# Self-attention of a transformer block: four first-pass banks, and row sums inverted in a layout over all partitions

## What is computed

```python
xn = layer_norm(x, ln0_w, ln0_b)
q, k, v = split(xn @ qkv_w.T)              # each as 16 heads x 32
attn = einsum('bhnd,bhmd->bhnm', q, k) * 32 ** -0.5
attn = softmax(attn)                       # 2048 keys a row
sa = merge(einsum('bhnm,bhmd->bhnd', attn, v)) @ sa_proj_w.T
x = x + sa
```

## Time and profile before

| | |
|---|---|
| median of 3 runs | 3681.93 us (3677.66 to 3685.92) |
| the profiled execution | 3683.99 us, its span 3682.2 us |
| TensorE (PE) busy | 3365.0 us, 91% of the span |
| VectorE (DVE) busy | 2215.5 us, 60% |
| GpSimd (POOL) busy | 1701.3 us, 46% |
| ScalarE (ACT) busy | 1545.2 us, 42% |
| maxima, L1591 | 2048 of 676 ns, 1277.9 us |
| exponentials, L1549 | 2048 of 603 ns, 1068.0 us |
| pair sums, L1397 | 192 of 4598 ns and 64 of 4579 ns |
| accumulating DMAs, L1402 | 128 of 1024 KB, 7.2 us to landing |

### The profile page before, as it was taken

One profiled execution on the slowest core, in us unless ns is written; L12 is line 12 of the kernel. 1 busy time (PEld: TensorE's weight loads), 2 busy tenths in 40 slices (PEclk: granted clock), 3 DMA queues, 4 the chain that ended last, 5 costly groups with the idle time before them and its releaser, 6 DMA issues. The chain is left out here.

```text
span 3682.2 us, 52183 instructions
## 1 busy us (share of the span) xinstructions
PE 3365.0 (91%) x16432; PEld 2104.9 (57%) x16432; DVE 2215.5 (60%) x3731; ACT 1545.2 (42%) x2794; POOL 1701.3 (46%) x507
## 2 busy tenths in 40 slices
PE   7998999999999999999999668898876689999999
PEld 6885544444444444444444156556535568888887
DVE  4445878887888888888888125666644632222222
ACT  3230666666666666666666512442422321111111
POOL 0001788888888888888878622342322200000000
PEclk9997999999999999999999887898957889999999
DMA  4547347465465746546553453333315741111110
GB/s 171 180 163 183 71 100 161 87 133 116 96 131 107 155 86 140 115 97 131 107 118 74 106 146 95 116 112 108 90 53 206 263 163 46 46 46 46 46 46 23
DMA packets 178499, 412.01 MB, mean 112 GB/s; under 512 B 20289, under 2 KB 43399, under 8 KB 158831
## 3 DMA queue, kind: packets, MB, share of 16 engines
q1 hardware_dynamic: 156271, 273.87, 24.4%
q0 software_dynamic: 18432, 134.23, 18.2%
q10 hardware_dynamic: 3584, 1.05, 0.1%
HBM read 146.08 MB, written 102.56 MB: 68 GB/s over the span
## 5 line engine op out<-in xcount | busy, mean ns | idle before, releaser
L1591 DVE TENSOR_REDUCE self_part_max<-self_first 128x1 f32<-128x512 f32 x2048 | 1277.9, 676 | 299.9 <-PE self_first L1448 296.6
L1549 ACT ACTIVATE self_expo<-self_second 128x512 f32<-128x512 f32 x2048 | 1068.0, 603 | 690.0 <-PE self_second L1464 656.4
L1397 POOL TENSOR_TENSOR self_pair_sum<-self_expo 128x2048 f32<-128x2048 f32 x192 | 882.8, 4598 | 117.4 <-ACT self_expo L1549 93.9
L1448 PE MATMUL self_first<-self_k,self_q 96*128 96x512 f32 x2048 | 884.6, 439 | 40.9 <-DVE self_part_max L1591 24.2
L1464 PE MATMUL self_second<-self_q,self_k 98*128 98x512 f32 x2048 | 813.4, 400 | 13.5 <-ACT self_expo L1549 13.4
L1448 PEld LDWEIGHTS self_first<-self_k,self_q 96*128 96x128 f32 x2048 | 394.6, 193 | 559.1 <-DVE self_part_max L1591 445.2
L1477 PE MATMUL self_weighted<-self_expo,self_v_sb 128*32 128x512 f32 x4096 | 546.3, 605 | 9.1 <-ACT self_unscaled L1561 6.9
L1464 PEld LDWEIGHTS self_second<-self_q,self_k 98*128 98x128 f32 x2048 | 388.5, 190 | 109.6 <-ACT self_expo L1549 47.7
L1943 DVE CAST mlp_h_high<-mlp_h 128x512 fp32r<-128x512 f32 x128 | 54.7, 427 | 505.6 <-PE mlp_out_sum L61 504.6
L1918 ACT ACTIVATE mlp_h<-mlp_hidden_sum,mlp_b_col 128x512 f32<-128x512 f32 x128 | 88.0, 688 | 601.1 <-PE mlp_hidden_sum L61 601.1
L1397 POOL TENSOR_TENSOR self_half_sum<-self_expo 128x2048 f32<-128x2048 f32 x64 | 292.7, 4579 | 82.9 <-ACT self_expo L1549 82.9
(11 more groups left out here) (165 smaller groups left out, 4130.7 us busy)
## 6 DMA issues: line engine op xcount, KB each, us to landing
self_half_sum<-self_pair_sum POOLq DMA_DIRECT2D x128, 1024.0 KB, 7.2
self_k<-k_t SPq DMA_DIRECT2D x96, 256.0 KB, 9.7
self_q<-q_t SPq DMA_DIRECT2D x93, 256.0 KB, 4.5
cross_q<-cross_r_high SPq DMA_DIRECT2D x256, 64.0 KB, 2.0
qkv_x<-in_x SPq DMA_DIRECT2D x8, 1024.0 KB, 5.4
v<-qkv_v_sb SPq DMA_DIRECT2D x32, 256.0 KB, 2.0
q_t<-qkv_r_high SPq DMA_DIRECT2D x32, 256.0 KB, 2.0
q_t<-qkv_r_low SPq DMA_DIRECT2D x32, 256.0 KB, 2.3
```

The source lines that it names most:

```text
L1397: nc.gpsimd.tensor_tensor(to, expo[:, t % p_slots], expo[:, (t + 1) % p_slots], ALU.add).then_inc(pair_done, 1)
L1448: nc.tensor.matmul(first[:, in_ring[n]], q[0:base, c % q_slots, a, s * P:(s + 1) * P], k[0:base, c // stages_per_group % 2, a, k0:k0 + TOK ...
L1549: nc.scalar.activation(expo[:, t % p_slots, a], second[:, n % ring], ACT.Exp, scale=scale).then_inc(exp_done, 1)
L1591: nc.vector.tensor_reduce(part_max[:, a * SUB + s, k:k + 1], first[:, in_ring[n]], AX_X, ALU.max).then_inc(first_read, 1)
```

## The change

It has three parts.

1. **Banks.** The first pass gets four banks (`f_ring`), the second keeps three (`s_ring`), `weighted` keeps one, and `total` has none of its own. The transposed maximum and `total` now take slots of the second pass's ring (`s_uses` lists the ring's uses in order; `second_free` waits for the use three places back). The transpose stands between first-pass items 0 and 1 (`turn_after = 1`).
2. **Sums.** The three sums stand in a row behind block 3. ScalarE copies `weighted` straight into `mean` (block 1, once the last `mean` is stored) and `total` into `inverse` in SBUF (`take_total`, behind exponential 15). Since sums and overwritten buffers have moved, GpSimd's `part_sum` has four parts whose roles alternate by stage.
3. **Inversion.** One row of each head is sent by four small DMAs from `inverse` into `sums`, a tensor of 128 partitions x 16 columns (`send_sums`). VectorE inverts that in one instruction in block 7. SyncE stores it to DRAM (`spread_inverse`), waits for this, and loads each head's 512 values into 32 partitions of `inverse` by a broadcast DMA, four in all. VectorE divides in block 11: `inverse` times `mean`, both in SBUF. SyncE then stores `mean`.

The maxima's two DMAs stay behind block 13 (`max_sent_after = 55`).

```diff
-    turn_after = 2
-    ring = 3
+    turn_after = 1
+    f_ring = 4
+    s_ring = 3
...
-    sums_at = {15: [(0, 0)], 2: [(-1, 1)], 3: [(-1, 2)]}
-    last_sum, invert_from, max_sent = 3, 5, 13
+    sum_block, take_sum_after = 3, 4 * per_block - 1
+    invert_at, divide_at, max_sent_after = (7, 1), (11, 1), 55
...
+    s_uses = []
+    for j in range(blocks):
+        for at in range(per_block):
+            if first_of[j][at] == (2, turn_after - 1):
+                s_uses.append("turn")
+            s_uses.append(j * per_block + at)
+        if j == sum_block:
+            s_uses.append("total")
+    s_slot = {use: p % s_ring for p, use in enumerate(s_uses)}
...
-        first = m.psum("first", [P, ring, TOK])
-        second = m.psum("second", [P, ring, TOK])
+        first = m.psum("first", [P, f_ring, TOK])
+        second = m.psum("second", [P, s_ring, TOK])
         weighted = m.psum("weighted", [P, TOK])
-        total = m.psum("total", [P, TOK])
+        total = second[:, s_slot["total"]]
+        turned_max = second[0:n_max, s_slot["turn"], 0:P]
...
+                def send_sums(i):
+                    ge(sp, total_read, i + 1, alone=True)
+                    for a in range(heads):
+                        rows = slice(a * HEAD_DIM, (a + 1) * HEAD_DIM)
+                        sp.dma_start(sums[rows], inverse[a * HEAD_DIM:a * HEAD_DIM + 1].rearrange("o (j k) -> o j k", k=share)
+                                     ).then_inc(sums_loaded, 16)
+
+                def spread_inverse(i):
+                    ge(sp, inverse_done, i + 1, alone=True)
+                    sp.dma_start(inverse_rows.rearrange("a (j k) -> (a j) k", k=share), sums[:]).then_inc(inverse_stored, 16)
+                    ge(sp, inverse_stored, 16 * (i + 1), alone=True)
+                    for a in range(heads):
+                        sp.dma_start(inverse[a * HEAD_DIM:(a + 1) * HEAD_DIM],
+                                     inverse_rows[a].unsqueeze(0).to_broadcast([HEAD_DIM, TOK])).then_inc(inverse_loaded, 16)
...
+                    if number != 0:
+                        send_sums(i - 1)
                     v_free(0)
                     if number != 0:
+                        spread_inverse(i - 1)
+                    v_free(1)
+                    if number != 0:
                         store_out(r, c - 1)
-                    v_free(1)
                     v_free(2)
...
+                def take_total(i):
+                    ge(act, total_done, n_sums * (i + 1))
                     ge(act, mean_done, i)
-                    nc.scalar.activation(unscaled[:], weighted[:], ACT.Copy).then_inc(weighted_read, 1)
+                    nc.scalar.activation(inverse[:], total, ACT.Copy).then_inc(total_read, 1)
...
+                def invert(i):
+                    ge(dve, sums_loaded, 16 * heads * (i + 1))
+                    nc.vector.reciprocal(sums[:], sums[:]).then_inc(inverse_done, 1)
 
                 def divide(i):
-                    ge(dve, inverse_done, pieces * (i + 1))
+                    ge(dve, inverse_loaded, 16 * heads * (i + 1))
                     ge(dve, weighted_read, i + 1)
-                    ge(dve, out_stored, 16 * i)
-                    nc.vector.tensor_tensor(mean[:], total[:], unscaled[:], ALU.mult).then_inc(mean_done, 1)
+                    nc.vector.tensor_tensor(mean[:], inverse[:], mean[:], ALU.mult).then_inc(mean_done, 1)
```

More of the change, by code:

```diff
@@ L1197, in self_phase @@
     n_seconds = heads * n_k
-    blocks = n_k
-    per_block = heads
+    blocks = 16
+    per_block = n_seconds // blocks
     firsts_per_block = n_items // blocks
     ahead = per_head
-    turn_after = 2
-    ring = 3
+    turn_after = 1
+    f_ring = 4
+    s_ring = 3
     p_slots = 8
-    pieces = 8
+    share = heads * TOK // P
     k_set = n_k // 4
@@ L1213, in self_phase, with sum_parts @@
     n_adds = n_pairs + 1
[L1214 to L1215 removed]
+    sum_block, take_sum_after = 3, 4 * per_block - 1
+    invert_at, divide_at, max_sent_after = (7, 1), (11, 1), 55
     items = [(a, s, k0) for a in range(heads) for s in range(SUB) for k0 in range(0, keys, TOK)]
[L1218 to L1240 removed]
+    def sum_parts(c):
+        return (0, 1, 2, 3) if c % 2 == 0 else (2, 1, 0, 3)
     first_of = [[] for _ in range(blocks)]
@@ L1381, in _ @@
                     period(rounds - 1, c)
+                send_sums(stages - 1)
+                spread_inverse(stages - 1)
                 store_out(rounds - 1, round_stages - 1)
@@ L1461, in second_pass @@
                         ge(pe, max_loaded, 32 * (i + 1))
-                    held = n - ring if n >= ring else (n_seconds - 1 - n) // ring * ring + n - n_seconds
-                    ge(pe, exp_done, n_seconds * i + held + 1)
-                    nc.tensor.matmul(second[:, n % ring],
+                    second_free(i, n)
+                    nc.tensor.matmul(second[:, s_slot[n]],
                                      k[0:exp_rows, c // stages_per_group % 2, a, t * P:(t + 1) * P],
@@ L1503, in batch @@
                             weigh(r, c - 1, t + n_k)
-                    for of, n in sums_at.get(j, ()):
-                        if with_this if of == 0 else with_last:
-                            add_up(round_stages * r + c + of, n)
+                    if j == sum_block and with_last:
+                        add_up(r, c - 1)
                 def period(r, c, with_last, with_next, with_after):
@@ L1534, in _ @@
                     period(rounds - 1, c, True, c < round_stages - 1, c < round_stages - 2)
-                for j in range(last_sum + 1):
+                for j in range(sum_block + 1):
                     batch(rounds - 1, round_stages, j, True, False)
@@ L1579, in _ @@
                 take_weighted(stages - 1)
+                take_total(stages - 1)
             @block.vector
@@ L1642, in _ @@
                 period(stages - 1, True, False, False)
-                for part in range(pieces):
-                    invert(stages - 1, part)
+                invert(stages - 1)
                 divide(stages - 1)
```

180 lines of the change are left out of this document (93 added, 87 removed).

## The result

The changed kernel takes 3709.52 us (median of 8 runs, 3703.61 to 3731.09), the kernel before beside it 3684.64 us. The ratio is 1.0063, with an interval of 1.0039 to 1.0086: it is slower by 14 to 32 us, where 15 us were forecast (3697 against 3681.93). The profiled execution took 3709.01 us, its span 3707.2 us. One execution among the experiments, of the kernel without the store and the loads, took 4223.91 us at a mean granted clock of 0.73; its ratio leaves it out.

What follows compares the result with a forecast made beforehand. The prediction took TensorE to bound the self-attention phase. Its terms, -10.2 + 21 - 3 + 7.7 = +15.5 us on the profiled 3683.99, gave 3699.5, forecast as 3697 us since the runs' median is 2.1 lower; range 3667 to 3842.

Steps and rivals of the forecast that it cites:

- Part 1: In the block with the transpose the fourth bank ends a wait of TensorE: 0.34 us saved a stage, -10.2 us.
- Part 2: The three sums, now one after another, cost their blocks the same wherever they stand: 0.
- Part 3, the race: Store of the inverse against the stage's first accumulation: store goes first, lands 2.3 us after issue; margin some 0.2 us.
- The lost race: Rival, chance 0.27: the store lands late, the sixth addition holds the division 5.75 us a stage; +158, or 3840 us.
- Part 3, +0.7 us a stage: Division in block 11 waits for GpSimd's fifth addition, until A+12.8 (A: issue of the stage's first accumulating DMA); +21 us.
- Part 4: The maxima's two DMAs on ScalarE: the second's issue still stalls, but 0.1 us is saved a stage, -3 us.
- Part 5: End of the phase, behind the last sum: copy, small DMAs, reciprocal, store and loads precede the division; +7.7 us.
- The reciprocals cost TensorE nothing: In the self-attention stages, blocks take 3.05 us with a VectorE reciprocal and 3.05 us without one.

Runs made afterwards that it cites:

- made by hand: Changed kernel with the small reciprocal one block later, so the store of the inverse leaves inside the running accumulation: 3933.61 us, ratio 1.067.

## Why the prediction came out as it did

The direction, the mechanism and the place are right: the division with both inputs in SBUF is held until GpSimd's fifth addition is done, and the row maximum and the transpose wait behind it. Step by step:

- **Part 1, -0.34 us a stage.** Without a hold the block is 3.98 us (no store and loads) against 4.23: -0.25, so the sign and three quarters of the size. What is late next is not only the row maximum, but also the split behind one maximum.
- **Part 2, 0.** Right for the sums (a block of 5.64 us, 2.57 above a plain one, against three of 3.93, each 0.87 above). Wrong by 3.8 us for what the sum in block 15 had covered, the landing of the maxima's DMA. I had costed the move at 0 and named no cover for the place that it left.
- **Part 3, the race.** The store landed after 1.4 us and not 2.3, in each stage (1.7 in the first); its first packets moved 0.85 us after its issue, those of the accumulation 1.44 us after theirs, so the margin was some 0.45 us. The lost race, which had a chance of 0.27, came in no stage; made by hand, its mechanism and place are right and its time 94 us too low.
- **Part 3, +0.7 us a stage.** The landing of the accumulation was put at 8.0 us; its median is 7.76, so the fifth addition ends at A+12.47 in most stages and the hold is 0.28 us. That is less than half of the term. But in six stages the landing was 8.2 to 9.1, the hold 1.3 us or more, and those six stages make some 19 of the 21.9 us that the two blocks grew. **The step that failed is the use of one middle value** for a time that varies from stage to stage, where the loss grows faster than the hold: a hold of 0.86 us (stage 28) made the block 0.87 us longer than without one, and holds of 1.3 us or more cost 2.7 to 4.5 us in the two blocks.
- **The clock.** No term of the sum had it. In those six stages TensorE works at 1.2 GHz for 3.4 or 6.8 us around or behind its stop; the stage at 675, whose row maximum was 1.3 us later than in most stages, paid 4.0.
- **Part 4, -3 us:** measured -3.3.
- **Part 5, +7.7 us:** measured +5.9; the small DMAs took 1.4 and 1.7 us to land where I had allowed 2.3.
- **"The reciprocals cost TensorE nothing"** is right for plain blocks, but not for the block with the transpose, where they cost 0.18 us a stage.
- **The total.** Against the profiled execution +15.5 us were forecast and +25.0 came. The phase alone cost more: +21.9 for the two blocks of parts 1 and 3 (+10.8 forecast), +5.0 for part 2's blocks (0 forecast), -3.3, +5.9, and +1.7 in all other blocks are +31.2, twice the sum. The phases around it, whose code is the same, gave 5.8 us back in this execution; I take that for chance, and the forecast looks the better for it.

The Trainium skill's rule ("SBUF — State Buffer", "Who interferes with whom") named the hold and its condition. The trace before had one meeting; the pair of kernels that differ in one operand shows that the condition is the second SBUF input (682 against 3619 ns). Of "the first to start wins" the runs show one half: 30 of 30 divisions began inside the addition and ended behind it. No run has an unhindered division begin first, so the other half isn't shown.

## What to carry to other kernels

Before an operand is moved from PSUM to SBUF on VectorE, look at what GpSimd does at that moment; a multiplication of 0.7 us can last until a 4.6 us addition is done. Put such an instruction where nobody waits behind it, and judge the slot by the latest landing in the trace and not by the mean, since a stop of TensorE of 2.07 us cost 4.4 us here. Ask of each moved instruction also what it covered where it stood.

## What the runs showed of the hardware

- VectorE's `tensor_tensor` of 128x512 took 0.68 us beside an addition of GpSimd with one input in PSUM, and ended 0.55 us behind the addition with both in SBUF, whether 0.4 or 3.5 us of it were left. Reciprocals of 128x64 from SBUF were not held (542 ns inside an addition and outside).
- A store of 8 KB issued 0.14 us behind a 1 MB accumulation landed after 1.4 us; issued 3.2 us behind it, after 3.9 us. Loads of 64 KB took 2.0 us ahead of one and 5.7 inside it.
- With nothing from SyncE beside it the first accumulation of a stage landed after 6.9 us in most stages of the kernel before, and after 7.9 to 9.15 us in two stages there and in five of the kernel without the store and the loads. All seven had a packet of 8 or 16 KB of an instruction queue in their time; 17 that landed after 6.9 to 7.7 us had one too. Whether it is the cause is open.
- The second of two DMA issues on ScalarE took 1.4 us in the middle of an accumulation, 3.5 us behind its issue as well as 1.5 us behind it (up to 2.4 us in some stages), and mostly 0.61 us from 5.6 us behind it on.
